# A product moved from VectorE to GpSimd and two mask matmuls from TensorE to VectorE, once in each of eight attention units

## The chip, the cores and the metric

The kernel runs on one core of a Trainium2 chip. The metric is the device time of one execution in microseconds (us); a comparison rests on the median of several runs. TensorE multiplies matrices, VectorE and GpSimd work elementwise, ScalarE does exponentials and copies, SyncE issues transfers. The engines run side by side and wait for one another through semaphores.

## What is computed

A block with a sparse or dense attention, a feed-forward layer, a second layer with an expert chosen per batch row, and a mixture of the best two of eight experts. Only the attention matters here. With these inputs it takes the sparse way, and every query's 32 key numbers lie below 256:

```python
Kg = K[:, :, idx]; Vg = V[:, :, idx]                       # 32 keys for each of 1024 queries
s_scores = jnp.einsum('bhsd,bhskd->bhsk', Q, Kg) * scale
s_scores = jnp.where(prior_index_mask[:Ss][None, None], s_scores, -jnp.inf)
sparse_out = jnp.einsum('bhsk,bhskd->bhsd', jax.nn.softmax(s_scores, axis=-1), Vg)
...
x = x + ffn(cond(x, ...))          # first layer
x = x + moe(experts(x, ...))       # second layer
```

Two batch rows, 1024 queries each, 16 heads of 16 numbers.

## The kernel before

The gather is turned into counting: for each query `few_W` holds how often each of the 256 keys occurs in its list (transposed, 128 keys on the partitions, two tiles of 1024 queries, bf16), and the probabilities are exp(score) times that count. `Mneg` is -1e30 where a count is zero (queries on the partitions, bf16); it keeps such keys out of the greatest score of a query.

The attention is cut into 8 units (2 batch rows x 4 groups of 4 heads), each with 8 jobs. `due()` (class `Few`) yields one list of steps that every engine goes through in the same order, each doing its own part. A job number counts for two kinds of work at different times. Guard job i, at time t = i, takes 128 queries and 4 heads: TensorE writes the scores of 2 heads x 256 keys into each of two banks of psG (L567) and adds `Mneg` with a second matmul against the unit matrix (L569); VectorE takes the negated maximum per head and query from each bank (L812) into column 48 of `few_Qa`. Bank p of guard i can be written when VectorE has reduced bank p of guard i - 1 (semaphore `g_max`; the first twelve guards use psS in turn with psG). Score job n, at time t = n + 12 (`LAG`), takes one head and one tile of 128 keys against 1024 queries: TensorE (L584) into psS, ScalarE's exp into slot n % 8 of `Pr` (L732), VectorE's "weigh" step (L820), which caps at 3e38 and multiplies by the counts in one instruction. The weigh step of job n - 1 stands in the list right after the guard of time t = n + 12. The values matmuls (L597), which read four slots of `Pr` at once, stand five jobs later ("values0", "values1").

So time t = 13 + 8u holds both guard 5 of a unit and the weigh step of the first job of unit u, one behind the other on VectorE.

Other work at these places: ScalarE's copy of the transposed queries (L724), which frees a bank of psM for TensorE's transposes (L618, L634); ScalarE's copies into `few_Qa` (L673, L674) and GpSimd's subtraction behind them (L440, step "fill"), twice in a unit; the normalization by VectorE once a unit (L830, L833); splits of weights into two parts on VectorE between the jobs (L1610); and GpSimd's L1902 near the end of the attention.

## Time and profile before

| | |
|---|---|
| median of 3 timed runs | 491.25 us (491.18 to 492.18) |
| profiled execution | 490.34 us, span 488.5 us, mean granted TensorE clock 0.994 |
| TensorE busy | 94% of the span |
| VectorE busy | 79% |
| ScalarE busy | 54% |
| GpSimd busy | 20% |
| attention: guards and scores | about 45 to 222 us of the span |

Rows of the trace give the start in us from the span's start, the duration, the engine (PE is TensorE, DVE is VectorE, ACT is ScalarE, POOL is GpSimd), the line, the operation and its operands (output<-inputs), and in brackets the idle time before with what ended it. xN means N instructions in a row. Ends of matmuls are modelled, so their starts are the better guide.

### The profile page before, as it was taken

The page shows a single profiled execution, that of the slowest core. Times are in us where ns is not written, and L with a number is a line of the kernel's source. Part 1 is how long each engine was busy: PE and PEld are TensorE (multiplying, and loading weights), DVE is VectorE, ACT ScalarE, POOL GpSimd, SP SyncE. Part 2 cuts the span into 40 slices and gives each one's busy share as a digit, 9 for nine tenths or more (in the row PEclk, how much of TensorE's full clock was granted, in tenths as well). Part 3 has the DMA queues.
Part 4 walks back from the last instruction along what each step waited for, and adds up shares of the span by engine and source line. Part 5 has one row for each costly group of instructions (what it writes and reads, how often), then busy time and mean ns, then how long its engine had stood idle before and what let it go on. Part 6 is the DMA issues. An engine that isn't in the chain of part 4 may idle for free.

```text
span 488.5 us, 7690 instructions
## 1 busy us (share of the span) xinstructions
PE 458.8 (94%) x2511; PEld 319.2 (65%) x2511; DVE 386.3 (79%) x760; ACT 261.4 (54%) x513; POOL 97.6 (20%) x102
## 2 busy tenths in 40 slices
PE   6999899999999999889999999999999999999990
PEld 3545554454555545436888888888888878899980
DVE  7998899999899989885976677657873779375376
ACT  4026588678769785874544544355343524465400
POOL 1003101101110122000100013300440024067744
PEclk9999999999999999999999999999999999999997
DMA  7700020999500000002241211111010102646357
GB/s 232 216 1 0 1 87 1 347 315 329 171 1 0 2 2 0 1 3 84 60 125 43 88 43 43 45 44 44 33 56 1 43 26 75 163 150 190 128 198 271
DMA packets 21536, 44.74 MB, mean 92 GB/s; under 512 B 7938, under 2 KB 14722, under 8 KB 21218
## 3 DMA queue, kind: packets, MB, share of 16 engines
q1 hardware_dynamic: 18850, 36.93, 24.3%
q0 software_dynamic: 2640, 7.24, 4.1%
q8 instruction: 24, 0.39, 0.4%
q14 instruction: 22, 0.18, 0.1%
HBM read 34.76 MB, written 23.00 MB: 118 GB/s over the span
## 4 chain that ended last, share of the span: by engine, by line
PE 71%; DVE 17%; ACT 3%; issue 3%; DMA 2%; POOL 1%; SPq 1%; DVEq 0%; ACTq 0%; POOLq 0%
DVE few_Qa L812 8%; PE psG L1697 5%; PE psG L1699 5%; PE psG L1698 5%; PE psS L1697 5%; PE psS L1699 5%; PE psS L1698 5%; PE psO L597 4%; DVE Pr L820 4%; PE psS L584 4%; PE psG L567 3%; PE psO L488 3%; PE psG L569 3%; PE psO L1697 2%; PE psO L1698 2%
## 5 line engine op out<-in xcount | busy, mean ns | idle before, releaser
L732 ACT ACTIVATE Pr<-psS 128x512 f32<-128x512 f32 x128 | 69.9, 602 | 33.2 <-PE psS L584 32.7
L820 DVE SCALAR_TENSOR_TENSOR Pr<-Pr,few_W 128x1024 f32<-128x1024 f32 x64 | 80.5, 1265 | 2.2 <-ACT Pr L732 2.1
L812 DVE TENSOR_REDUCE few_Qa<-psG 128x2 fp32r<-128x512 f32 x116 | 74.3, 681 | 5.6 <-PE psG L569 5.3
L567 PE MATMUL psG<-few_KG,QG 128*128 128x512 f32 x116 | 53.0, 500 | 3.1 <-DVE few_Qa L812 3.1
L584 PE MATMUL psS<-few_QAT,few_KP 128*128 128x512 f32 x128 | 48.1, 451 | 4.4 <-ACT Pr L732 2.9
L1960 DVE TENSOR_TENSOR hT_lo<-V,hT_hi 128x512 fp32r<-128x512 f32 x64 | 44.5, 695 | 2.2
L569 PE MATMUL psG<-Mneg,few_identb 128*128 128x512 bf16 x116 | 45.2, 390 | 0.0
L1958 DVE CAST hT_hi<-V 128x512 fp32r<-128x512 f32 x64 | 27.5, 429 | 19.7 <-ACT V L1883 12.6
L440 POOL TENSOR_TENSOR few_Qa<-Qn,few_Qa 128x256 fp32r<-128x256 f32 x16 | 16.4, 1025 | 124.9 <-ACT few_Qa L674 124.9
L584 PEld LDWEIGHTS psS<-few_QAT,few_KP 128*128 128x128 f32 x128 | 20.6, 189 | 26.7 <-issue 19.9
L1902 POOL TENSOR_TENSOR cT_lo<-attT,cT_hi 128x1024 fp32r<-128x1024 f32 x4 | 10.6, 2653 | 130.7 <-ACT cT_hi L1833 130.7
L1930 POOL DMA_INDIRECT expert_results<-block_out,block_rows x31 | 30.1, 971 | 26.6 <-ACT block_out L1864 19.6
L597 PE MATMUL psO<-Pr,few_VA 128*17 128x512 f32 x256 | 33.5, 598 | 0.4 <-DVE Pr L820 0.4
L567 PEld LDWEIGHTS psG<-few_KG,QG 128*128 128x128 f32 x116 | 22.3, 192 | 9.8 <-issue 7.1
L784 DVE TENSOR_SCALAR few_EQ<-few_idxb,cst 128x1024 f16<-128x1024 f16 x64 | 26.7, 476 | 1.8 <-ACT few_idxb L267 1.1
L569 PEld LDWEIGHTS psG<-Mneg,few_identb 128*128 128x128 bf16 x116 | 11.1, 96 | 25.3 <-issue 21.7
L1924 POOL DMA_INDIRECT expert_rows<-crow,place_in x24 | 25.0, 1041 | 7.7 <-issue 5.5
L1958 DVE CAST cT_hi<-V 128x512 fp32r<-128x512 f32 x8 | 3.4, 426 | 29.0 <-ACT V L1891 29.0
L724 ACT CAST few_QAT<-psM 128x512 fp32r<-128x512 f32 x32 | 19.1, 596 | 7.8 <-PE psM L552 7.8
L552 PE MATMUL psM<-cst,few_Qa 128*128 128x128 f32 x128 | 19.4, 274 | 0.5 <-DVE few_An L833 0.4
L1891 ACT ACTIVATE V<-psG,cbias 128x512 f32<-128x512 f32 x6 | 4.1, 689 | 26.4 <-PE psG L1699 26.4
L552 PEld LDWEIGHTS psM<-cst,few_Qa 128*128 128x128 f32 x128 | 15.6, 141 | 4.0 <-issue 2.0
(315 smaller groups left out, 1162.1 us busy)
## 6 DMA issues: line engine op xcount, KB each, us to landing
expert_rows<-blank_dram SPq DMA_DIRECT2D x8, 1548.0 KB, 24.0
block_rows<-expert_rows SPq DMA_DIRECT2D x31, 129.0 KB, 2.5
back<-expert_results SPq DMA_DIRECT2D x6, 512.0 KB, 6.7
staged<-w_dram SPq DMA_DIRECT2D x4, 512.0 KB, 4.5
x1T<-xT_dram SPq DMA_DIRECT2D x4, 512.0 KB, 4.0
staged<-ew_dram SPq DMA_DIRECT2D x4, 512.0 KB, 3.5
out_dram<-attT SPq DMA_DIRECT2D x6, 256.0 KB, 3.2
few_idxb<-entries_by_query SPq DMA_DIRECT2D x8, 128.0 KB, 4.3
```

The lines of the kernel that those rows point to most:

```text
L552: mm = nc.tensor.transpose(ps[:, p * 256 + j * P:p * 256 + j * P + P], self.Qa[:, f % SLOTS, st + j, 2 * p:2 * p + 2, :].rearrange("p h a ...
L567: nc.tensor.matmul(o, QG[:, (u // 2) % 2, st * P:st * P + P], self.KG[:, u % 2, 2 * p:2 * p + 2, :], start=True, stop=False)
L569: mm = nc.tensor.matmul(o, self.identb[:, :], Mneg[:, None, st * FEW_KEYS:(st + 1) * FEW_KEYS].to_broadcast([P, 2, FEW_KEYS]), start=False ...
L584: mm = nc.tensor.matmul(psS[:, f, :], self.KP[:, u % 2, j, r * P:r * P + P], self.QAT[:, u % 2, j // 2, q], start=True, stop=True)
L597: mm = nc.tensor.matmul(psO[VW * j:VW * j + VC, part, :], self.VA[:, b, r, h * VC:h * VC + VC], Pr[:, HG * r + j, 512 * part:512 * part + ...
L732: nc.scalar.activation(Pr[:, i % JOBS, 512 * f:512 * f + 512], psS[:, f, :], ACT.Exp, scale=SCALE).then_inc(self.s["s_exp"], 1)
L812: nc.vector.tensor_reduce(self.Qa[:, f % SLOTS, st, 2 * p:2 * p + 2, 48], self.guard_bank(i)[0][:, p, :].rearrange("p (h t) -> p h t", h=2 ...
L820: nc.vector.scalar_tensor_tensor(pr, pr, FMAX, self.W[:, r, :], ALU.min, ALU.mult).then_inc(self.s["s_prob"], 1)
L1697: nc.tensor.matmul(ps, w[0], a[1], start=start, stop=False)
L1698: nc.tensor.matmul(ps, w[1], a[0], start=False, stop=False)
L1699: return nc.tensor.matmul(ps, w[0], a[0], start=False, stop=stop)
L1960: nc.vector.tensor_tensor(tile.lo[at], v, tile.hi[at].bitcast(F32), ALU.subtract).then_inc(d["parts"], 1)
```

## The change

In each unit GpSimd does the weigh step of the first job, as two instructions: a minimum with 3e38 in place, then the product with the counts. The second waits for the first by a semaphore. The values matmuls wait for GpSimd's semaphore as well as VectorE's. And in the guards whose number is 5 modulo 8 TensorE leaves out the mask matmuls; VectorE adds `Mneg` and takes the maximum in one operation per head, four in a guard.

```diff
+BY_POOL = 0
+MASKED_BY_DVE = 5
+def weighed_before(n):
+    return n - (n + JOBS - 1 - BY_POOL) // JOBS
...
+                    if what == "weigh" and i % JOBS == BY_POOL:
+                        u = i // JOBS
+                        pool.wait_ge(self.s["s_exp"], 2 * (i + 1))
+                        pr = Pr[:, i % JOBS, :]
+                        nc.gpsimd.tensor_scalar(pr, pr, FMAX, None, ALU.min).then_inc(self.s["s_least"], 1)
+                        pool.wait_ge(self.s["s_least"], u + 1)
+                        nc.gpsimd.tensor_tensor(pr, pr, self.W[:, i % JOBS // HG, :],
+                                                ALU.mult).then_inc(self.s["s_prob_pool"], 1)
...
-                            nc.tensor.matmul(o, QG[:, (u // 2) % 2, st * P:st * P + P],
-                                             self.KG[:, u % 2, 2 * p:2 * p + 2, :], start=True, stop=False)
+                            mm = nc.tensor.matmul(o, QG[:, (u // 2) % 2, st * P:st * P + P], self.KG[:, u % 2, 2 * p:2 * p + 2, :],
+                                                  start=True, stop=st == MASKED_BY_DVE)
+                            if st == MASKED_BY_DVE:
+                                mm.then_inc(self.s["g_scores"], 1)
+                                continue
...
-                        pe.wait_ge(self.s["s_prob"], HG * (i + 1))
+                        pe.wait_ge(self.s["s_prob"], weighed_before(HG * (i + 1)))
+                        if r == BY_POOL // HG:
+                            pe.wait_ge(self.s["s_prob_pool"], u + 1)
...
+                            if i % JOBS == MASKED_BY_DVE:
+                                for h in range(2):
+                                    seen = self.guard_bank(i)[0][:, p, h * FEW_KEYS:(h + 1) * FEW_KEYS]
+                                    mm = nc.vector.tensor_tensor_reduce(
+                                        seen, seen, Mneg[:, MASKED_BY_DVE * FEW_KEYS:(MASKED_BY_DVE + 1) * FEW_KEYS], -1.0, FMAX,
+                                        ALU.add, ALU.min, self.Qa[:, f % SLOTS, st, 2 * p + h, 48:49])
+                                mm.then_inc(self.s["g_max"], 1)
+                                continue
...
-                    if what == "weigh":
+                    if what == "weigh" and i % JOBS != BY_POOL:
```

How the order of instructions changes. VectorE, around the sixth guard of a unit in the middle of the attention, before:

```order
L830 RECIPROCAL few_rden<-psM 128x32
L833 TENSOR_TENSOR few_An<-psM,few_rden 128x8x64
L812 TENSOR_REDUCE few_Qa<-psG 128x2 x2
L820 SCALAR_TENSOR_TENSOR Pr<-Pr,few_W 128x1024
L812 TENSOR_REDUCE few_Qa<-psG 128x2 x2
L820 SCALAR_TENSOR_TENSOR Pr<-Pr,few_W 128x1024
L812 TENSOR_REDUCE few_Qa<-psG 128x2 x2
L820 SCALAR_TENSOR_TENSOR Pr<-Pr,few_W 128x1024
```

The same place now (an ISA row with psG is one masked reduction, the one behind it writes its accumulator):

```order
L867 TENSOR_TENSOR few_An<-psM,few_rden 128x8x64
L846 TENSOR_REDUCE few_Qa<-psG 128x2 x2
L854 SCALAR_TENSOR_TENSOR Pr<-Pr,few_W 128x1024
L841 ISA psG,few_Qa<-psG,Mneg 128x256
L841 ISA few_Qa 128x1
L841 ISA psG,few_Qa<-psG,Mneg 128x256
L841 ISA few_Qa 128x1
L841 ISA psG,few_Qa<-psG,Mneg 128x256
L841 ISA few_Qa 128x1
L841 ISA psG,few_Qa<-psG,Mneg 128x256
L841 ISA few_Qa 128x1
L846 TENSOR_REDUCE few_Qa<-psG 128x2 x2
```

Two maxima and the product behind them have become eight instructions, and the next maxima follow at once.

GpSimd, in the attention (way21 is ScalarE's semaphore for the copies into few_Qa, way28 that of the exponentials, way31 that of the minimum), before:

```order
L440 TENSOR_TENSOR few_Qa<-Qn,few_Qa 128x16x16 [waits way21] x16
L1902 TENSOR_TENSOR cT_lo<-attT,cT_hi 128x1024 [waits at_hi]
L1902 TENSOR_TENSOR cT_lo<-attT,cT_hi 128x1024 [waits at_hi,attention_done]
```

And now, from the fifth unit's pair to the end:

```order
L452 TENSOR_SCALAR Pr<-Pr 128x1024 [waits way28]
L454 TENSOR_TENSOR Pr<-Pr,few_W 128x1024 [waits way31]
L459 TENSOR_TENSOR few_Qa<-Qn,few_Qa 128x16x16 [waits way21] x2
L452 TENSOR_SCALAR Pr<-Pr 128x1024 [waits way28]
L454 TENSOR_TENSOR Pr<-Pr,few_W 128x1024 [waits way31]
L459 TENSOR_TENSOR few_Qa<-Qn,few_Qa 128x16x16 [waits way21]
L1936 TENSOR_TENSOR cT_lo<-attT,cT_hi 128x1024 [waits at_hi]
L452 TENSOR_SCALAR Pr<-Pr 128x1024 [waits way28]
L454 TENSOR_TENSOR Pr<-Pr,few_W 128x1024 [waits way31]
L452 TENSOR_SCALAR Pr<-Pr 128x1024 [waits way28]
L454 TENSOR_TENSOR Pr<-Pr,few_W 128x1024 [waits way31]
L1936 TENSOR_TENSOR cT_lo<-attT,cT_hi 128x1024 [waits at_hi,attention_done]
```

The pairs stand behind a subtraction each, in the seventh unit behind the product for cT_lo.

TensorE, from the scores of slot 5 to the guard of slot 6 in a unit, before:

```order
L639 MATMUL psM<-cst,few_Kn 128x128 x2
L567 MATMUL psG<-few_KG,QG 128x512
L569 MATMUL psG<-Mneg,few_identb 128x512
L567 MATMUL psG<-few_KG,QG 128x512
L569 MATMUL psG<-Mneg,few_identb 128x512
L634 MATMUL psM<-cst,Qn 128x128 x4
L584 MATMUL psS<-few_QAT,few_KP 128x512 x2
L567 MATMUL psG<-few_KG,QG 128x512
```

And now:

```order
L663 MATMUL psM<-cst,few_Kn 128x128 x2
L586 MATMUL psG<-few_KG,QG 128x512 x2
L658 MATMUL psM<-cst,Qn 128x128 x4
L606 MATMUL psS<-few_QAT,few_KP 128x512 x2
L586 MATMUL psG<-few_KG,QG 128x512
```

The two masks are gone; the transposes of Qn (in other units of An) follow the guard directly.

## Rows read from the trace of the kernel before

**Rows 1.** The page's part 1: busy us, share of the span, instructions.

```profile
PE 458.8 (94%) x2511; PEld 319.2 (65%) x2511; DVE 386.3 (79%) x760; ACT 261.4 (54%) x513; POOL 97.6 (20%) x102
```

**Rows 2.** Busy time in one unit: stretch, length, engines, TensorE's clock, DMA.

```profile
134.80:156.14 21.34, 20.61 (x120) 10.89 (x120) 20.37 (x27) 16.57 (x37) 2.21 (x2) 1.00 0.00 1
```

**Rows 3.** The chain that ended last, at a unit's slots 0 and 1.

```profile
157.43 1.13 DVE Pr L820
...
159.31 0.47 PE psG L567
```

**Rows 4.** VectorE in order of time, slots 5, 6 and 0.

```profile
148.92 1.72 DVE L820 SCALAR_TENSOR_TENSOR Pr<-Pr,few_W 128x1024 f32<-128x1024 f32 x1
150.57 1.28 DVE L812 TENSOR_REDUCE few_Qa<-psG 128x2 fp32r<-128x512 f32 x2
151.77 1.21 DVE L820 SCALAR_TENSOR_TENSOR Pr<-Pr,few_W 128x1024 f32<-128x1024 f32 x1
...
156.14 1.29 DVE L812 TENSOR_REDUCE few_Qa<-psG 128x2 fp32r<-128x512 f32 x2 [0.60 <-PE psG L569]
...
177.60 1.29 DVE L812 TENSOR_REDUCE few_Qa<-psG 128x2 fp32r<-128x512 f32 x2 [0.22 <-PE psG L569]
```

**Rows 5.** TensorE in order of time, behind sixth guards of two units.

```profile
148.29 0.63 PE L634 MATMUL psM<-cst,Qn 128*128 128x128 f32 x4 [0.42 <-ACT few_QAT L724]
...
149.46 0.39 PE L569 MATMUL psG<-Mneg,few_identb 128*128 128x512 bf16 x1
...
170.15 0.63 PE L618 MATMUL psM<-cst,few_An 128*128 128x128 f32 x4 [0.80 <-ACT few_QAT L724]
```

**Rows 6.** VectorE's small instructions in order of time, before the attention.

```profile
4.80 0.16 DVE L207 TENSOR_SCALAR lam<-lam 128x2 f32<-128x2 f32 x1
...
11.53 0.41 DVE L769 TENSOR_TENSOR few_Kn<-psO,Pr 128x256 f32<-128x256 f32 x1
```

**Rows 7.** GpSimd: a fill; L1902's count, shortest, median and longest ns.

```profile
1.42 0.95 POOL L255 MEMSET few_Ka<- 128x1024 f32 x1
L1902 POOL TENSOR_TENSOR cT_lo<-attT,cT_hi x4: 2402/2412/3385, 189.4 to 341.2; 128x1024 fp32r<-128x1024 f32 x4
```

**Rows 8.** GpSimd in the attention, and VectorE's longest product.

```profile
138.67 1.48 POOL L440 TENSOR_TENSOR few_Qa<-Qn,few_Qa 128x256 fp32r<-128x256 f32 x1 [9.46 <-ACT few_Qa L674]
148.83 0.74 POOL L440 TENSOR_TENSOR few_Qa<-Qn,few_Qa 128x256 fp32r<-128x256 f32 x1 [8.68 <-ACT few_Qa L674]
170.69 1.31 POOL L440 TENSOR_TENSOR few_Qa<-Qn,few_Qa 128x256 fp32r<-128x256 f32 x1 [9.21 <-ACT few_Qa L674]
189.45 3.38 POOL L1902 TENSOR_TENSOR cT_lo<-attT,cT_hi 128x1024 fp32r<-128x1024 f32 x1 [6.51 <-ACT cT_hi L1833]
191.72 2.19 DVE L820 SCALAR_TENSOR_TENSOR Pr<-Pr,few_W 128x1024 f32<-128x1024 f32 x1
```

**Rows 9.** GpSimd's subtractions for few_Ka and a VectorE addition at the same time.

```profile
39.20 2.52 POOL L447 TENSOR_TENSOR few_Ka<-few_Kn,few_Ka 128x512 fp32r<-128x512 f32 x2 [36.56 <-DVE few_EQ L784]
40.31 0.42 DVE L765 TENSOR_TENSOR Qn<-psO,Pr 128x256 f32<-128x256 f32 x1 [0.92 <-PE psO L488]
```

**Rows 10.** The first two units: TensorE, VectorE and GpSimd in order of time.

```profile
59.86 0.69 PE L584 MATMUL psS<-few_QAT,few_KP 128*128 128x512 f32 x2 [1.34 <-DVE few_Qa L812]
64.45 0.74 POOL L440 TENSOR_TENSOR few_Qa<-Qn,few_Qa 128x256 fp32r<-128x256 f32 x1 [7.32 <-ACT few_Qa L674]
68.73 1.28 DVE L812 TENSOR_REDUCE few_Qa<-psG 128x2 fp32r<-128x512 f32 x2
74.22 0.46 PE L567 MATMUL psG<-few_KG,QG 128*128 128x512 f32 x1 [0.47 <-DVE few_Qa L812]
84.20 1.21 DVE L1610 TENSOR_TENSOR w_lo<-staged,w_hi 128x1024 fp32r<-128x1024 f32 x1
```

**Rows 11.** TensorE at guard 62, and VectorE at the attention's end.

```profile
191.35 0.47 PE L567 MATMUL psG<-few_KG,QG 128*128 128x512 f32 x1 [0.33 <-DVE few_Qa L812]
216.18 1.23 DVE L820 SCALAR_TENSOR_TENSOR Pr<-Pr,few_W 128x1024 f32<-128x1024 f32 x1 [0.24 <-ACT Pr L732]
```

More of the change, by code:

```diff
@@ L188, in bass_adaln_ffn @@
             "qg_full", "qg_out", "kt_full", "kt_out", "kg_ready", "k_copied", "k_twice", "ka_ready", "ka_full", "kp_out",
-            "q_hi", "q_lo", "g_scores", "g_max", "qa_full", "qat_out", "s_scores", "s_exp", "s_prob",
+            "q_hi", "q_lo", "g_scores", "g_max", "qa_full", "qat_out", "s_scores", "s_exp", "s_prob", "s_prob_pool", "s_least",
             "pv_done", "ot_out", "on_full", "recip", "on_out", "at_full", "at_out")
@@ L805, in vector @@
                         f, st = divmod(i, HALF)
+                        if i == MASKED_BY_DVE:
+                            dve.wait_ge(self.s["neg_out"], 2)
                         if f >= SLOTS and st % 2 == 0:
```

## The prediction

> **What bounds the kernel now.** I read the page's busy shares first, then the stretches, then the chain, then single engines. TensorE is busy 94% of the span, VectorE 79%, GpSimd 20% [rows 1]. The edit touches only the attention stage, from about 45 us to 222 us, and there the picture is closer: one unit of eight jobs lasts 21.34 us, in which TensorE is busy 20.61 us and VectorE 20.37 us [rows 2]. Two engines share the bound, coupled by the two psG banks: a guard matmul needs the bank that VectorE has reduced one job before. I call the eight jobs of a unit slots 0 to 7, by the guard that stands in them. The chain shows who is late where [rows 3]: VectorE in slot 0 (maxima, the product of 157.43 us) and the first half of slot 1 (one maximum, in the row left out), which releases TensorE at 159.31 us; from there to the next such place TensorE and ScalarE set the pace. The edit lies in slot 5: the product of a unit's first job and its sixth guard stand next to each other. VectorE reaches TensorE again only where it waits for it, 0.60 us before slot 0 in one unit and 0.22 us in the next [rows 4]. That slack is what the added work of slots 5 to 7 may use for nothing.
>
> **TensorE: two mask matmuls fewer in each unit.** A mask matmul lasts 0.39 us with its modelled end [rows 5], so at most 0.78 us of work goes, less since matmuls overlap. Nothing of it is a gain: right behind the sixth guard TensorE waits for ScalarE's copy of QAT, 0.42 us in one unit and 0.80 us in the next [rows 5], and that copy hangs on exponentials issued before the guard. The wait gets longer by what the masks took. Value 0, eight times. Were that wait not there, the gain would be at most 8 x 0.78 = 6.2 us.
>
> **VectorE: four masked reductions in place of two.** Two maxima take 1.20 us from start to start (150.57 to 151.77 [rows 4]). Each new instruction adds 128x256 from PSUM and from SBUF, and has a second instruction behind it that writes the accumulator. The nearest row for the first part is an addition of 128x256 from PSUM, 0.41 us; for the second, an instruction of 128x2, 0.16 us [rows 6]. So a pair costs between 0.41 us (each overlaps its predecessor by 0.08 us, as products do, 1.21 us long for a step of 1.13) and 0.57 us (each waits for the other); below nothing is out, since twice as many instructions go over as many elements. I take 0.50 us, the middle: 2.0 us for 1.20, **+0.8 us** in slot 5 (+0.4 to +1.1).
>
> **VectorE: one product fewer.** A product starts the next instruction 1.13 us later [rows 3]: **-1.13 us** in slot 5. Slot 5 gets 0.3 us shorter on VectorE.
>
> **GpSimd: two instructions more, and what they hold up.** In a unit's slot 5 they stand behind the subtraction for Qa (0.74 us [rows 8]). The second, a product of two SBUF inputs of 128x1024, has a very near row: L1902, 2.41 us in the median [rows 7]. The first, a minimum with a constant, isn't in the trace. The nearest rows are GpSimd's MEMSET of 128x1024, 0.95 us, which writes the same amount and reads nothing, and that product with one read more, 2.41 us [rows 7]. I take 1.0 us: the extra of the product over the fill seems to be its two reads. Ends 0.95 and 2.4 us. The wait of the second on the first I leave at nothing; it covers itself with the step to the next instruction.
> By time alone GpSimd is free for this: the values of a unit's first half come five jobs later, over 12 us, and the pair needs under 6. The price is elsewhere. Rows show that GpSimd's elementwise instructions and VectorE's products exclude one another: L1902, issued at 189.45 us just behind a product, took 3.38 us, and the product of 191.72 us took 2.19 us where the one of 151.77 us took 1.21 [rows 4]; the subtraction of 138.67 us took 1.48 us for 0.74 [rows 8]. A VectorE addition with one input in PSUM and one in SBUF wasn't held up beside GpSimd (0.42 us at 40.31 us, while GpSimd subtracts from 39.20 to 41.7 us [rows 9]), so maxima and masked reductions run on. The Trainium skill (SBUF — State Buffer, Who interferes with whom) says the same as a rule: a VectorE instruction with two SBUF inputs and a GpSimd instruction that reads SBUF block each other for a whole instruction, whichever comes first; the trace agrees (2.19 us). A sum that left it out would give VectorE 0.3 us back in each slot 5.
>
> **One unit, walked through** (before's times, around 148.8 us). The subtraction starts at 148.83 us and ends at 149.57 [rows 8]; minimum to 150.6, product to 153.0 us. VectorE: masked reductions 147.7 to 149.7; the maxima of slot 6 wait for TensorE's masks (the first of them runs from 149.46 to 149.85 us [rows 5]) and run from about 149.95 to 151.15. Now its product wants to start, and GpSimd holds it till 153.0. Then product, maxima, product: 153.0 + 1.13 + 1.20 + 1.13 = 156.45 us, where slot 0's maxima began at 156.14 [rows 4]: **+0.3 us**. In the other kind of unit (subtraction at 170.69 us, slot 0 at 177.60 [rows 4, 8]) the same walk is 170.69 + 0.74 + 1.0 + 2.41 + 3.46 = 178.3 us: **+0.7 us**. Slot 0 is on the chain, so both pass on whole. Third to sixth unit: 0.3 + 0.7 + 0.3 + 0.7 = **+2.0 us**.
>
> **The other places.**
> - Guard 5 (sixth of the first unit, before any product): maxima follow each other without a gap there and TensorE's first scores wait 1.34 us for them [rows 10]. **+0.8 us**, whole.
> - First unit, slot 5: VectorE has no gap here. Subtraction at 64.45 us, GpSimd's product ends at 64.45 + 0.74 + 1.0 + 2.41 = 68.6, VectorE's product at 69.7, while the next maxima began at 68.73 us. TensorE waits for VectorE at 74.22 us [rows 10]. **+1.0 us**.
> - Second unit: no gap either, and a split of weights (84.20 us [rows 10]) in slot 5, two SBUF inputs too, so the order is open. VectorE pays +0.8 - 1.13, a hold of 1.2 us (GpSimd's product begins with the maxima) to 2.4 us, and saves the 0.5 us for which the subtraction held a product here (as at 148.92 us, 1.72 long [rows 4]): +0.4 to +1.6. I take **+1.0 us**.
> - Seventh unit: TensorE waits 0.33 us for the first maximum of guard 61 [rows 11]; the first bank now comes free 2 x 0.50 - 0.60 = 0.4 us later, the second 0.8. **+0.6 us**. The 0.98 us that L1902 cost a product falls away with that product, but behind TensorE.
> - Last unit: VectorE has gaps here; GpSimd's product delays those of jobs 58 to 61; by a walk like the one above, the one that began at 216.18 us [rows 11] starts at 216.5: **+0.3 us**, before a VectorE stretch without gaps.
>
> Sum: 0.8 + 1.0 + 1.0 + 2.0 + 0.6 + 0.3 = **+5.7 us**. The profiled execution took 490.34 us (span 488.5), so 496.0 us; it lay 0.9 us under the median of the three timed runs. Against that median, 491.25 us, the forecast is **497.0 us**.
>
> **Rivals.**
> - A, the lock falls the other way: GpSimd's minimum takes over 1.55 us, so VectorE's product of slot 6 is issued before GpSimd's. Then GpSimd's product runs under the maxima of slot 7 and costs what the slack covers; walked as above: product of slot 6 from 151.15 us, GpSimd's from 152.3 to 154.7, product of slot 7 to 155.85, before 156.14 (no loss); in the other kind of unit it comes out at 177.7 for 177.60 (+0.1). The four middle units cost 0.2 in place of 2.0; the gapless ones about 1 each as before: +0.8 + 2.0 + 0.2 + 0.6 + 0.3 = +3.9, or 495.1 us; with cheap reductions (0.40 us a pair) 494. For it: the minimum has no row of its own. Against: its nearest row is 0.95 us.
> - B, **faster**: GpSimd's new instructions don't hold VectorE's products, and the accumulator pairs cost 0.40 us. Then slot 5 pays in the two gapless units, 2 x (-1.13 + 0.4) = -1.5 us, and the second unit's hold by the subtraction goes, -0.5; guards 5 and 61 cost 0.4 + 0.2. That is -1.4 us, 489.9 us against the median. It turns at a hold of some 0.7 us in each gapless unit. Against: the three holds of [rows 8]; for: none of them is by a GpSimd instruction with one input.
> - C, no change: no holds, but pairs of 0.50 us: 2 x (-1.13 + 0.8) - 0.5 + 0.8 + 0.6 = +0.2 us, 491.5 us. For and against as in B.
> - D, the accumulator pairs are dear: 0.75 us each. Then each slot 5 grows by 1.8 us, guard 5 costs 1.8, and TensorE's guard of slot 6 waits as well: about +10, 501 us. Against: an addition of 128x256 takes 0.41 us [rows 6].
> On A's open price there is a page: the Trainium skill (GPSIMD Engine Reference, Elementwise — side-by-side cycle accounting) gives 1.03 cycles per element at 1.2 GHz for short bodies, an estimate of 0.88 us for the minimum, and by it the middle units would cost 0.5 us less. No row of before shows it.
>
> **Chances.** Forecast (GpSimd first, 495 to 499.5 us with the ends of the unknown prices) 0.53; A 0.20; D 0.07; C 0.09; B 0.11. What a measurement of this kernel can tell from no change is about 0.2%, 1.0 us. Faster 0.11, same 0.09, slower 0.80. The range, 491 to 500 us, leaves out B and the top of D.
>
> **What would show it.** In the changed kernel's trace: (1) TensorE's wait for ScalarE's QAT copy behind the sixth guard near 0.9 and 1.25 us; (2) four masked reductions in 2.0 us; (3) GpSimd's minimum near 1.0 us and product near 2.4; (4) in slot 6 a VectorE product of some 3 us with GpSimd's beside it; (5) units of 21.7 to 22.1 us. A minimum above 1.55 us and a held product in slot 7 would be A; no long product anywhere would be B and prove the forecast wrong; so would units of 21.4 us in spite of the holds, if TensorE's chain turned out to be later than I read it.

## The result, and the profile after

The changed kernel takes 493.12 us (median of 22 runs, 491.86 to 495.51), the kernel before beside it 491.30 us (22 runs). The ratio is 1.0029, with a 95% interval of 1.0017 to 1.0041: slower, by 1.4 us (0.8 to 2.0; the two medians lie 1.8 us apart). The direction was forecast and the time lies in the range, but the forecast was +5.7 us.

To see where the time goes I measure the same places in each profile from one common start, VectorE's first maxima of the attention (45.28 us before, 45.20 us after), to its last pair of weight splits (217.33 us before). That is the whole attention stage, without what lies ahead of it and behind it. All "landmarks" below are such distances, taken from VectorE's rows in order of time.

```profile
45.20 1.28 DVE L846 TENSOR_REDUCE few_Qa<-psG 128x2 fp32r<-128x512 f32 x2
...
218.69 2.35 DVE L1644 TENSOR_TENSOR w_lo<-staged,w_hi 128x1024 fp32r<-128x1024 f32 x2
```

After: 218.69 - 45.20 = 173.49 us; before: 172.05 us. So the profiled attention stage got 1.44 us longer, which agrees with the timed runs. The two profiled executions as a whole differ by more, 490.34 and 493.69 us: another 2.0 us lie behind the last landmark, where the code is the same (more on it below). Landmarks in between (the maxima of guard 12 at 61.13 us before, the start of guard 21 at 83.00 us before, the reciprocal of each unit) divide the stage. The masks of guard 21, +0.29 us, count to the second unit, in whose slot 5 they stand:

| place | forecast | after less before |
|---|---|---|
| guard 5 | +0.8 | +0.30 |
| first unit | +1.0 | +0.28 |
| second unit | +1.0 | +0.18 |
| third to sixth unit | +2.0 | +0.03 |
| seventh unit | +0.6 | +0.25 |
| last unit | +0.3 | +0.40 |
| sum | +5.7 | +1.44 |

Part 1 of the page of after, answering to [rows 1] (busy us, share, instructions):

```profile
PE 456.5 (93%) x2495; PEld 317.9 (65%) x2495; DVE 382.6 (78%) x800; ACT 261.9 (53%) x513; POOL 139.4 (28%) x118
```

TensorE has 2.3 us less to do, VectorE 3.7 us less, and the kernel is slower. GpSimd has 41.8 us more. The unit in the middle, VectorE in order of time, the place of [rows 4] (CUSTOM_DVE_ANT_0 is a masked reduction, the row behind it writes its accumulator):

```profile
148.43 0.43 DVE L841 CUSTOM_DVE_ANT_0 psG<-psG,Mneg 128x256 f32<-128x256 f32 x1
148.77 0.14 DVE L841 DVE_READ_ACCUMULATOR2_ANT few_Qa<- 128x1 fp32r x1
148.77 0.47 DVE L841 CUSTOM_DVE_ANT_0 psG<-psG,Mneg 128x256 f32<-128x256 f32 x1
...
150.64 1.29 DVE L846 TENSOR_REDUCE few_Qa<-psG 128x2 fp32r<-128x512 f32 x2 [0.59 <-PE psG L591]
151.85 1.21 DVE L854 SCALAR_TENSOR_TENSOR Pr<-Pr,few_W 128x1024 f32<-128x1024 f32 x1
153.80 1.29 DVE L846 TENSOR_REDUCE few_Qa<-psG 128x2 fp32r<-128x512 f32 x2 [0.74 <-PE psG L591]
155.01 1.32 DVE L854 SCALAR_TENSOR_TENSOR Pr<-Pr,few_W 128x1024 f32<-128x1024 f32 x1
156.82 1.29 DVE L846 TENSOR_REDUCE few_Qa<-psG 128x2 fp32r<-128x512 f32 x2 [0.49 <-PE psG L591]
```

and GpSimd at the same place:

```profile
149.53 0.74 POOL L459 TENSOR_TENSOR few_Qa<-Qn,few_Qa 128x256 fp32r<-128x256 f32 x1 [8.68 <-ACT few_Qa L698]
150.24 2.77 POOL L452 TENSOR_SCALAR Pr<-Pr 128x1024 f32<-128x1024 f32 x1
153.09 2.15 POOL L454 TENSOR_TENSOR Pr<-Pr,few_W 128x1024 f32<-128x1024 f32 x1
```

Three things to read here. The masked reductions step by 0.38 us, not 0.50. GpSimd's minimum takes 2.77 us, not 1.0, and lies outside both of my ends (0.95 and 2.4). And VectorE's product of slot 6 starts at 151.85 us, 1.6 us after that minimum has begun, and takes 1.21 us as ever: the minimum isn't holding it. By the time GpSimd's product starts (153.09), VectorE's is out, and the two maxima of slot 7 run under it. Only the end of GpSimd's product touches VectorE's next one, 1.32 us in place of 1.21. VectorE then waits 0.49 us for TensorE at slot 0. This is the order of the rival A.

In the first two units VectorE has hardly a gap (two waits for TensorE of 0.2 us each in the first), and there products are held. VectorE in slots 6 and 7 of the second unit, and GpSimd beside it:

```profile
86.13 1.28 DVE L846 TENSOR_REDUCE few_Qa<-psG 128x2 fp32r<-128x512 f32 x2
87.33 1.56 DVE L854 SCALAR_TENSOR_TENSOR Pr<-Pr,few_W 128x1024 f32<-128x1024 f32 x1
88.81 1.28 DVE L846 TENSOR_REDUCE few_Qa<-psG 128x2 fp32r<-128x512 f32 x2
90.01 2.83 DVE L854 SCALAR_TENSOR_TENSOR Pr<-Pr,few_W 128x1024 f32<-128x1024 f32 x1
```

```profile
86.77 2.77 POOL L452 TENSOR_SCALAR Pr<-Pr 128x1024 f32<-128x1024 f32 x1
89.62 2.14 POOL L454 TENSOR_TENSOR Pr<-Pr,few_W 128x1024 f32<-128x1024 f32 x1
```

The product of 90.01 us is held until GpSimd's has ended (89.62 + 2.14 = 91.76; it is done 1.1 us later). The product of 87.33 us starts 0.56 us into the minimum and is 0.35 us longer than 1.21: held up to 0.9 us into a minimum of 2.77 us, and not to its end at 89.54 us. That second kind of hold is the news of this case.

TensorE behind the sixth guard, the place of [rows 5]:

```profile
148.99 0.63 PE L658 MATMUL psM<-cst,Qn 128*128 128x128 f32 x4 [0.88 <-ACT few_QAT L748]
...
170.84 0.63 PE L642 MATMUL psM<-cst,few_An 128*128 128x128 f32 x4 [1.25 <-ACT few_QAT L748]
```

0.42 and 0.80 us have become 0.88 and 1.25 us: the masks that TensorE no longer does turned into a wait for ScalarE, as forecast.

### The profile page after: what moved, and what is told of

Its sections match the earlier page's. It is cut to its first block, busy times and chain, and to the rows that moved or that the text cites. A ratio compares the mean times of both kernels' runs of the same rounds, so it can differ in the third digit from the quotient of the medians.

```text
span 491.9 us, 7729 instructions
## 1 busy us (share of the span) xinstructions
PE 456.5 (93%) x2495; PEld 317.9 (65%) x2495; DVE 382.6 (78%) x800; ACT 261.9 (53%) x513; POOL 139.4 (28%) x118
## 4 chain that ended last, share of the span: by engine, by line
PE 71%; DVE 17%; issue 3%; ACT 3%; DMA 2%; POOL 2%; SPq 0%; DVEq 0%; ACTq 0%; POOLq 0%
DVE few_Qa L846 7%; PE psG L1731 5%; PE psG L1733 5%; PE psG L1732 5%; PE psO L621 5%; PE psS L1731 5%; PE psS L1733 4%; PE psS L1732 4%; DVE Pr L854 4%; PE psS L606 4%; PE psG L586 3%; PE psO L507 3%; PE psG L591 3%; PE psO L1731 2%; PE psO L1732 2%
## 5 line engine op out<-in xcount | busy, mean ns | idle before, releaser
L854 DVE SCALAR_TENSOR_TENSOR Pr<-Pr,few_W 128x1024 f32<-128x1024 f32 x56 | 73.5, 1320 | 1.8 <-ACT Pr L756 1.7
L846 DVE TENSOR_REDUCE few_Qa<-psG 128x2 fp32r<-128x512 f32 x102 | 65.5, 683 | 10.7 <-PE psG L591 10.6
L586 PE MATMUL psG<-few_KG,QG 128*128 128x512 f32 x116 | 51.5, 491 | 4.1 <-DVE few_Qa L846 3.4
L591 PE MATMUL psG<-Mneg,few_identb 128*128 128x512 bf16 x102 | 39.7, 390 | 0.0
L606 PEld LDWEIGHTS psS<-few_QAT,few_KP 128*128 128x128 f32 x128 | 20.6, 189 | 27.6 <-issue 20.8
L1958 POOL DMA_INDIRECT expert_rows<-crow,place_in x24 | 26.3, 1096 | 7.7 <-issue 5.5
L452 POOL TENSOR_SCALAR Pr<-Pr 128x1024 f32<-128x1024 f32 x8 | 22.8, 2856 | 9.2 <-ACT Pr L756 9.2
L591 PEld LDWEIGHTS psG<-Mneg,few_identb 128*128 128x128 bf16 x102 | 9.7, 96 | 22.1 <-issue 19.9
```

The lines of the kernel that those rows point to most:

```text
L586: mm = nc.tensor.matmul(o, QG[:, (u // 2) % 2, st * P:st * P + P], self.KG[:, u % 2, 2 * p:2 * p + 2, :], start=True, stop=st == MASKED_BY ...
L591: mm = nc.tensor.matmul(o, self.identb[:, :], Mneg[:, None, st * FEW_KEYS:(st + 1) * FEW_KEYS].to_broadcast([P, 2, FEW_KEYS]), start=False ...
L606: mm = nc.tensor.matmul(psS[:, f, :], self.KP[:, u % 2, j, r * P:r * P + P], self.QAT[:, u % 2, j // 2, q], start=True, stop=True)
L846: nc.vector.tensor_reduce(self.Qa[:, f % SLOTS, st, 2 * p:2 * p + 2, 48], self.guard_bank(i)[0][:, p, :].rearrange("p (h t) -> p h t", h=2 ...
L854: nc.vector.scalar_tensor_tensor(pr, pr, FMAX, self.W[:, r, :], ALU.min, ALU.mult).then_inc(self.s["s_prob"], 1)
```

## Experiments

Two questions: is the loss in the masks or in the product, and which of GpSimd's two instructions holds VectorE, for how long? Later a third: is there time in TensorE's masks anywhere else? The spans and landmarks are of one profiled execution each; the ratios are timed runs against the kernel before on the same chip.

### One half of the change at a time

```diff
-MASKED_BY_DVE = 5                      # pool_only: every mask by TensorE again
+def masked_by_dve(i): return False
```

> The product of each unit's first job by GpSimd (minimum, then product), the mask matmuls left with TensorE in all guards. Theory 1 (the holds fall where VectorE has slack: the minimum, 2.77 us in the changed kernel's trace, lets VectorE's product of slot 6 go first): the four middle units cost nothing, the first two about nothing to 0.4 us together, the last unit 0.4; VectorE's split of weights that began at 217.33 us before begins at 217.5 to 218.1; ratio 1.000 to 1.002. Theory 2 (the holds cost as much as was predicted, some 0.5 us a unit, and the masks that TensorE no longer does pay it back): units of 21.8 us, that split at 219.5 to 221, ratio 1.004 to 1.008.

```diff
-                    if what == "weigh" and i % JOBS == BY_POOL:    # mask_only: every product by VectorE
+                    if what == "weigh" and False:
```

> Only the masked reductions of each unit's sixth guard by VectorE, all products by VectorE. Theory 1: TensorE's saved matmuls lengthen its wait for the QAT copy and gain nothing; four pairs of 0.38 us for 1.20 cost 0.33 us each at guard 5 and in the two gapless units, 0.2 at guard 61, nothing in the middle: the split of 217.33 us at 218.2 to 218.5, ratio 1.001 to 1.003. Theory 2: TensorE's saving counts, 0.3 to 0.5 us a unit: the split at 214.5 to 216, ratio 0.993 to 0.998.

| | attention stage, less before | timed ratio (95%) |
|---|---|---|
| product only | +0.28 | 1.0022 (1.0004 to 1.0039) |
| masks only | +1.15 | 1.0052 (1.0039 to 1.0064) |
| both (the change) | +1.44 | 1.0029 (1.0017 to 1.0041) |

In the profiles the halves add up to the change (0.28 + 1.15 = 1.43). The masks cost 0.30 us at each of guard 5, the first and the second unit, nothing in the third to sixth and 0.25 us in the seventh. The product costs nothing before the last unit (0.09 us up to guard 21, -0.05 us up to the reciprocal behind it): in the gapless first two units the 1.13 us taken off VectorE and what GpSimd's two instructions hold cancel. In the last unit it costs 0.3 to 0.4 us. VectorE in pool_only, beside [rows 11]:

```profile
208.19 1.54 DVE L864 SCALAR_TENSOR_TENSOR Pr<-Pr,few_W 128x1024 f32<-128x1024 f32 x1 [0.44 <-ACT Pr L766]
210.31 7.71 DVE L864 SCALAR_TENSOR_TENSOR Pr<-Pr,few_W 128x1024 f32<-128x1024 f32 x5 [0.59 <-ACT Pr L766]
```

Five products in 7.71 us, where free ones, 1.13 us apart, would need 5.7: GpSimd's product (from 210.46 us, 3.08 long) falls among them. The 2.0 us more are covered for the most part, since before VectorE waits for ScalarE four times between its last products (as in [rows 11]).

The timed ratios of the halves are larger than their landmarks, by 0.8 and 1.4 us, and don't add up: 1.1 and 2.6 us for the halves, 1.4 us for both. The profiles show no such loss in the attention, and it stays open (more on it below, at the masks in slots 6 and 7). So the split between the halves rests on one profile of each.

### The minimum: left out, and cut short

```diff
-                        nc.gpsimd.tensor_scalar(pr, pr, FMAX, None, ALU.min).then_inc(self.s["s_least"], 1)
-                        pool.wait_ge(self.s["s_least"], u + 1)
```

> The changed kernel without GpSimd's minimum (the cap at 3e38 of these eight products is left out); its product follows the subtraction at once. Theory 1: the product of 2.14 us holds VectorE's product of slot 6 by some 0.5 us, which the wait for TensorE before slot 7 covers; in the first two units it holds less than in the changed kernel; the last unit's delay goes too. The split of 217.33 us (before), 218.69 (changed) at 216.8 to 217.8; ratio 0.998 to 1.001. If GpSimd's product costs by its mere 2.1 us of hold wherever it stands: 218.7 or later.

```diff
-                        nc.gpsimd.tensor_scalar(pr, pr, FMAX, None, ALU.min).then_inc(self.s["s_least"], 1)
+                        nc.gpsimd.tensor_scalar(pr[:, 0:352], pr[:, 0:352], FMAX, None, ALU.min).then_inc(self.s["s_least"], 1)
```

> The changed kernel with the minimum over 352 of 1024 columns, some 1.0 us as the prediction took it (the cap is left out for the other columns). It puts GpSimd's product back where the prediction had it, in front of VectorE's product of slot 6. The prediction's walk with the measured 2.14 us product: slot 0 later by 0.0 and 0.4 us in turn in the middle units, first unit +0.7, second +0.5, guard 5 +0.3: the split of 217.33 us at 219.0 to 220.5, ratio 1.003 to 1.007. If the order of the two products does not matter: as the changed kernel, 218.7 or less.

Without the minimum the attention stage is 0.30 us longer than before (+0.28 at guard 5, -0.07 and -0.17 in the first two units, +0.25 in the seventh, none in the last) and the ratio is 1.0003 (0.9984 to 1.0022). So the minimum makes 1.1 us of the change's 1.4, in the first, second and last unit.

Cut to 352 of 1024 columns it takes 1.09 us, nearly the 1.0 us that I had assumed, and the kernel gets much slower: attention stage +5.27 us, ratio 1.0148 (1.0120 to 1.0176). A shorter instruction costs more. VectorE and GpSimd in the middle unit of that kernel:

```profile
153.11 1.29 DVE L856 TENSOR_REDUCE few_Qa<-psG 128x2 fp32r<-128x512 f32 x2 [0.60 <-PE psG L601]
154.31 2.78 DVE L864 SCALAR_TENSOR_TENSOR Pr<-Pr,few_W 128x1024 f32<-128x1024 f32 x1
```

```profile
152.68 1.09 POOL L462 TENSOR_SCALAR Pr<-Pr 128x352 f32<-128x352 f32 x1
153.86 2.16 POOL L464 TENSOR_TENSOR Pr<-Pr,few_W 128x1024 f32<-128x1024 f32 x1
```

This is the picture that the prediction drew: GpSimd's product has gone first, and VectorE's product of slot 6 lasts 2.78 us. The third to sixth unit cost 0.07, 0.74, 0.04 and 0.73 us here, where the walk said 0.3 and 0.7 in turn. So the walk had the mechanism of this order right. That its size fits as well is in part luck: with the measured 2.14 us for GpSimd's product the same walk gives 0.0 and 0.4, as expected above, and 0.3 us of every second unit stay unexplained. The first unit costs 0.76 us (+1.0 forecast, +0.7 expected); the second gains 1.06, since there VectorE's product gets in first again (90.24 us, GpSimd's at 90.86). Most of the rest, 3.7 us, falls in the seventh unit and is a second race of the same kind. Before, GpSimd's L1902 starts 0.06 us after a product of VectorE (189.45 [rows 8], the product at 189.39 us) and waits for it. Here, VectorE and then GpSimd:

```profile
193.31 3.21 DVE L864 SCALAR_TENSOR_TENSOR Pr<-Pr,few_W 128x1024 f32<-128x1024 f32 x1
```

```profile
193.07 2.38 POOL L1946 TENSOR_TENSOR cT_lo<-attT,cT_hi 128x1024 fp32r<-128x1024 f32 x1 [7.68 <-ACT cT_hi L1877]
```

GpSimd is 0.24 us ahead; VectorE's product is held to 3.21 us, and TensorE behind it waits 2.52 us for psG, up to 197.45 us, where it waits 0.52 us in the changed kernel. That is 2.0 us. Right behind the wait TensorE's granted clock falls to half (third number from the end) for about 3.3 us:

```profile
198.00:199.00 1.00, 1.00 (x3) 0.55 (x3) 0.65 (x3) 0.00 (x0) 1.00 (x1) 0.50 0.00 0
200.00:201.00 1.00, 1.00 (x8) 0.15 (x8) 1.00 (x2) 0.00 (x0) 0.00 (x0) 0.50 0.00 0
```

From the matmul of 197.45 us to the next guard TensorE takes 4.92 us, for 3.45 in the changed kernel at full clock: another 1.5 us. Neither the prediction nor the expectation had either.

### A minimum running all the time

```diff
+                    if what == "weigh" and i < 44:          # the kernel before, and on GpSimd:
+                        pool.wait_ge(self.s["s_exp"], 2 * (i + 1))
+                        pool.wait_ge(self.s["idle"], i + 1)
+                        nc.gpsimd.tensor_scalar(self.idle[:, :], self.idle[:, :], FMAX, None, ALU.min).then_inc(self.s["idle"], 1)
```

> The kernel before, with a GpSimd minimum of an unused tile of 128x768 at the place of each of the first 44 weigh steps, so that such minima meet VectorE's products at many phases; nothing reads them. If GpSimd's one-input minimum holds VectorE's products only in a first part (0.9 us of 2.77 for 1024 columns in the changed kernel, so some 0.7 of 2.1 here), products that start later than 0.7 us into a minimum last 1.21 us, and the longest product is near 1.9 us. If it holds them for its whole length, products of up to 3.3 us appear and those that start late in a minimum are lengthened too. If it holds nothing, all are at 1.21 us but those beside the subtraction.

If a minimum held VectorE's products for its whole length, 44 of them close behind one another would lengthen the attention by far more than the 0.41 us that they cost over the whole stage. VectorE and GpSimd in a stretch where neither rests:

```profile
104.88 1.21 DVE L826 SCALAR_TENSOR_TENSOR Pr<-Pr,few_W 128x1024 f32<-128x1024 f32 x1
...
109.55 1.34 DVE L826 SCALAR_TENSOR_TENSOR Pr<-Pr,few_W 128x1024 f32<-128x1024 f32 x1
```

```profile
103.03 2.13 POOL L442 TENSOR_SCALAR few_idle<-few_idle 128x768 f32<-128x768 f32 x1 [0.15 <-POOL few_idle L442]
105.32 2.77 POOL L442 TENSOR_SCALAR few_idle<-few_idle 128x768 f32<-128x768 f32 x1 [0.16 <-POOL few_idle L442]
...
108.98 2.13 POOL L442 TENSOR_SCALAR few_idle<-few_idle 128x768 f32<-128x768 f32 x1
```

The product of 104.88 us starts 1.85 us into a minimum and takes 1.21 us. The one of 109.55 us starts 0.57 us into one and takes 1.34: held to 0.70 us into it. At 1024 columns the hold ended 0.9 us in (above). In this run eight products start within the first 0.6 us of a minimum, and each is held up to 0.68 to 0.70 us into it; those that start 0.73 to 2.27 us into one take 1.21 or 1.22 us. 0.70 / 768 and 0.9 / 1024 are both 0.9 ns a column, so at these two widths the hold is a third of the instruction. The other way round it works too: the minimum of 105.32 us starts within a product and takes 0.64 us longer. The durations (1.09 us for 352 columns, 2.13 for 768, 2.77 for 1024) make 2.5 ns a column and 0.2 us; GpSimd's product with two inputs needs 2.14 us for 1024. The instruction with one input less is the slower one, and holds VectorE the less.

The timed ratio is 1.0059 (1.0027 to 1.0090), 2.9 us, much more than 0.41. A part of that the profile shows: TensorE's granted clock in three stretches at the attention's end (TensorE's share of full speed is the third number from the end):

```profile
210.00:215.00 5.00, 4.02 (x22) 1.18 (x14) 4.02 (x4) 4.03 (x9) 0.00 (x0) 1.00 0.00 0
215.00:220.00 5.00, 4.59 (x20) 1.16 (x20) 4.51 (x5) 3.31 (x7) 0.00 (x0) 0.66 0.00 0
220.00:225.00 5.00, 5.00 (x32) 3.25 (x32) 3.96 (x6) 1.37 (x2) 0.00 (x0) 0.99 0.63 209
```

A clock of 0.66 over 5 us is 3.4 us at 1.2 in place of 2.4 GHz. The attention's end (first matmul of aoT_lo) then comes 1.53 us later than before, where the last split still was 0.41 late. The other 1.4 us of the timed 2.9 stay open.

### Masks where VectorE has slack

The change put the masks on VectorE in slot 5. In slots 6 and 7 VectorE waits before slot 0 (0.60 and 0.22 us [rows 4]), masked reductions cost only 0.38 us a head for 0.30, and what TensorE saves in slot 7 stands behind ScalarE's QAT copies. Both kernels are the kernel before with another set of guards:

```diff
+def masked_by_dve(i): return i in (31, 39, 47, 55)              # mask7_late
+def masked_by_dve(i): return i in (31, 38, 39, 47, 54, 55)      # mask_where_slack, slack_again
```

> Masked reductions by VectorE in guards 31, 39, 47 and 55 (slot 7 of the four units in which VectorE waits for TensorE there), nothing else changed. Theory 1 (what counts is the slot: behind slot 5's guard TensorE waits anyway, before slot 0 it is the later engine): slot 0 begins 0.47 us earlier in two units (no longer than TensorE's two masks) and about 0.2 us earlier in the other two, where VectorE is then the later one: attention 1.1 to 1.4 us shorter, ratio 0.997 to 0.998. Theory 3 (TensorE's masks never count, being hidden everywhere): attention unchanged or up to 1.3 us longer.

> As the last one, and guards 38 and 54 (slot 6 of the two units in which VectorE waits 0.41 us for TensorE there). Theory 1: 0.47 us in two units and 0.7 us in the other two, attention 2.0 to 2.4 us shorter, ratio 0.995 to 0.996. Theory 3: unchanged or up to 2 us longer.

The attention stage is 1.15 and 2.06 us shorter, as expected; with six guards the units last 20.8 and 20.95 us for 21.3 and 21.5. The timed ratios are 0.9996 (0.9976 to 1.0015) and 1.0001 (0.9985 to 1.0017): nothing, where 0.995 to 0.998 was expected. The profile of mask_where_slack, its clock in the same stretches as above:

```profile
210.00:215.00 5.00, 3.83 (x16) 1.33 (x16) 3.77 (x5) 4.03 (x9) 0.00 (x0) 0.99 0.00 0
215.00:220.00 5.00, 5.00 (x24) 1.50 (x24) 4.66 (x4) 2.48 (x5) 0.00 (x0) 0.67 0.02 7
```

Ahead of the fall TensorE had waited for ScalarE's exponentials three times, 0.23 to 0.60 us each, from 209.96 to 214.56 us. Up to the first matmul of aoT_lo the gain has shrunk from 2.06 to 1.02 us (mask7_late: from 1.15 to 0.08, with 0.86 and 0.80 in its two stretches). Before has the same waits and no fall. So I asked whether the fall belongs to the kernel and can be filled away, on another chip, with two spare mask matmuls into an idle psG bank where TensorE waits:

```diff
+                            if f == 0 and i in (57, 61, 62):
+                                pe.wait_ge(self.s["g_max"], 2 * UNITS * JOBS)
+                                for _ in range(2):
+                                    nc.tensor.matmul(psG[:, 0, :].rearrange("p (h t) -> p h t", h=2), self.identb[:, :],
+                                                     Mneg[:, None, 0:FEW_KEYS].to_broadcast([P, 2, FEW_KEYS]), start=True, stop=True)
```

> The kernel before, with two spare bf16 mask matmuls (128x512, about 0.23 us each from start to start) into an idle psG bank ahead of the score jobs 57, 61 and 62 of the last unit, where TensorE waits 0.57 to 0.61 us for ScalarE. Theory (the waits there come ahead of a fall of the granted clock in some executions): the mean granted clock rises from 0.991 and the time falls by up to 0.5 us. Rival (the clock has nothing to do with it): no change of clock, time equal within 0.2%. Both leave the attention's landmarks where they were (last w_lo pair 172.05 us after the first maxima, within 0.2).

> The masks of guards 31, 38, 39, 47, 54 and 55 on VectorE, and the spare matmuls. Without them this edit gained 2.06 us up to the last w_lo pair, and only 1.02 us up to the first matmul of aoT_lo, since TensorE's clock was granted at 0.50 from 215 to 218.8 us; timed it gained nothing. Theory (clock): no stretch at 0.50 near 215 us, the gain at aoT_lo is 1.8 to 2.1 us, mean clock 0.991 or more, time 0.3 to 0.4% under before. Rival (the gain is lost in the later stage, 400 us and on): clock cured, gain at aoT_lo 2 us, time still within 0.1% of before.

> The same masks without the spare matmuls, on the chip and beside the runs of the others. Clock theory: mean granted clock 0.0025 below before's again, time about 1 us above the version with spare matmuls, within 0.2% of before. Rival: the two versions are equal in time.

| | attention stage, less before | at aoT_lo | mean clock | timed ratio (95%) |
|---|---|---|---|---|
| spare matmuls only | -0.08 | -0.09 | 0.9912 | 1.0000 (0.9983 to 1.0016) |
| masks and spare matmuls | -2.15 | -2.15 | 0.9887 | 0.9977 (0.9964 to 0.9990) |
| masks again, without them | -2.14 | -2.14 | 0.9875 | 0.9977 (0.9958 to 0.9995) |

(The mean clock is of 12 runs each; the 35 runs of before beside them had 0.9895. This chip takes 499.45 us for the kernel before, 7 to 9 us more than the others, but the attention's landmarks of the first row are those of before within 0.1 us.) The very same kernel that showed the fall on the first chip has a full clock here:

```profile
215.00:220.00 5.00, 5.00 (x30) 3.14 (x28) 4.90 (x6) 1.77 (x3) 0.00 (x0) 1.00 0.35 104
```

and keeps its 2.14 us at the attention's end. So the fall is not fixed by the kernel's order. With and without the spare matmuls the time is equal: the clock theory's expectation (1 us between the two) failed, and so did the mean clock of 0.991 or more. The spare matmuls do nothing measurable to the time, though the mean clock is a little higher with them (0.9912 for 0.9895, 0.9887 for 0.9875). Whether they would fill away a fall was not tested: this chip's profile of the masks without them has none there. What stays of the mask edit is 0.23% on this chip (0.05 to 0.42%; 0.10 to 0.36% with the spare matmuls), half of the 2.1 us in the profile, and nothing measurable on the first one. It is still the one version here, with the next, that beat the kernel before anywhere.

The other half I can only place, not explain. From the last landmark to the end every kernel runs the same code, and the profiled executions differ there by up to 5 us (271.2 us before, 273.2 us in the changed kernel, 276.0 us in no_min; on the last chip all are longer). TensorE's first wait for the experts' rows, in mask_where_slack and in no_min:

```profile
419.13 0.41 PE L1791 MATMUL psM<-cst,block_rows 128*128 128x128 f32 x2 [1.01 <-DMA block_rows<-expert_rows]
```

```profile
418.79 0.41 PE L1789 MATMUL psM<-cst,block_rows 128*128 128x128 f32 x2 [1.69 <-DMA block_rows<-expert_rows]
```

Before, the largest such wait is 0.28 us, at 417.75 us, in the changed kernel 0.78 us, at 418.85 us, and up to the matmul for x_lo at 402 us nothing has changed since the attention's end (178.1 to 178.2 us in before, mask_where_slack and no_min). One profile of each can't say whether an earlier or later attention causes it, or chance. A lower clock is a second candidate: the mean granted clock of the masked kernels lies 0.0008 to 0.0027 under that of before beside them, on both chips. But the two versions on the last chip, with and without spare matmuls, differ by 0.0012 in it and not in time.

### The measured prices put together

```diff
+UNITS_OF_POOL = (2, 3, 4, 5)                                    # GpSimd's product in four units only
+def masked_by_dve(i): return i in (30, 31, 38, 39, 46, 47, 54, 55)
```

> The measured prices put to use: in the third to sixth unit GpSimd takes the first product (VectorE 1.13 us less, GpSimd's minimum 2.77 us, its product under the maxima of slot 7), and VectorE masks slots 6 and 7 there (8 pairs at 0.38 us, +0.66 us for the unit) where it had slack, so TensorE is 1.56 us of mask matmuls lighter; spare matmuls as before. Theory (two coupled engines, both must get lighter): units of 20.2 to 20.8 us for 21.27 and 21.53, the last w_lo pair 2.5 to 4 us earlier, time 0.4 to 0.8% under before. Rival (ScalarE's exponentials or the hold of VectorE's products by GpSimd's product end it): no better than 2.0 us at the w_lo pair.

The attention stage is 1.68 us shorter (units of 20.7 and 21.4 us), ratio 0.9972 (0.9953 to 0.9992): a gain, but less in the profile than with the masks alone (2.15), and not the 2.5 to 4 us that I expected. VectorE in slots 5 and 6 and TensorE there:

```profile
125.55 1.28 DVE L861 TENSOR_REDUCE few_Qa<-psG 128x2 fp32r<-128x512 f32 x2
128.21 0.43 DVE L856 CUSTOM_DVE_ANT_0 psG<-psG,Mneg 128x256 f32<-128x256 f32 x1 [1.38 <-PE psG L596]
...
132.44 1.60 DVE L869 SCALAR_TENSOR_TENSOR Pr<-Pr,few_W 128x1024 f32<-128x1024 f32 x1
```

```profile
126.71 0.63 PE L657 MATMUL psM<-cst,few_An 128*128 128x128 f32 x4 [0.80 <-ACT few_QAT L763]
```

The product taken off VectorE in slot 5 becomes a wait of 1.38 us, since TensorE stands before slot 6 waiting for ScalarE's QAT copy whatever VectorE does. Behind that wait come the dearer masked reductions and a product held by GpSimd's (1.60 us). The fourth and the sixth unit show it best: there the masked guards are those of the masks alone, and with GpSimd's product the gain falls from 0.6 to 0.2 us a unit. Here, work taken off an engine in front of a wait and put on it behind the wait is a loss. The rival's number held (no better than 2.0 us), and one of its two reasons, the hold by GpSimd's product, is there with 0.39 us; the other was the wrong work of ScalarE, the exponentials and not the QAT copy.

## Why the prediction was right or wrong

**Right.** The masks on TensorE are worth nothing where they were left out: the QAT wait grew to 0.88 and 1.25 us, as said (0.9 and 1.25). VectorE's maxima and masked reductions run on beside GpSimd. VectorE's and GpSimd's products exclude each other for nearly the whole instruction (2.83 us at 90.01 us, 2.78 us in the kernel with the short minimum: held up to 2.0 us into GpSimd's 2.14). The loss from masks at guard 5 and in the seventh unit, and from GpSimd in the last one, lies where it was said.

**Wrong, first of all: the minimum's price, and with it the order in slot 6.** The prediction took 1.0 us, with ends of 0.95 and 2.4 us. It was 2.77 us, above the upper end. The nearest row was chosen by the amount written (the MEMSET of [rows 7]), and the extra of the product was put down to its reads; the product with two reads as an upper end seemed safe, and was not. What decides is the length at which VectorE's product of slot 6 gets in ahead of GpSimd's, 1.55 us by the rival A, and the minimum lies beyond it. So the order is A's: middle units +0.03 us where the forecast said +2.0 and A +0.2. That is 2.0 of the 4.3 us by which the sum was too high. The kernel with a minimum of 1.09 us shows the forecast's order, and 1.58 us in those four units. That the measured time lies within 491 to 500 us is no merit of the walk: the range was wide enough to hold A and C as well.

**Wrong: that every elementwise instruction of GpSimd holds VectorE's products.** I let them be held with its whole length. The three holds of [rows 8] were all between instructions with two inputs, which rival B noted; the two cases without holds, B and C, I weighed at 0.20. The minimum holds for 0.9 us of 2.77. The Trainium skill (SBUF — State Buffer, Who interferes with whom) calls the shared pair of ports an exclusive lock, and says of VectorE's two-port modes that whoever issues first has it "for the whole instruction"; for the two products the trace agrees (2.0 of 2.14 us), for GpSimd's one-input minimum the measurement decides against it (0.9 of 2.77 us).

**Wrong in size.** A masked reduction with its second instruction steps by 0.38 us (148.77, 149.15, 149.53 us), below my lower end of 0.41: guard 5 cost +0.30 and not +0.8. GpSimd's product takes 2.14 us, not 2.41. First unit: -1.13 us for the product, +0.3 for the masks, one product held by 0.75 us (69.68 us, 1.96 long), a hold of 0.2 us by the subtraction that falls away (74.59 us before, 1.42 long), and some 0.6 us for the two waits for TensorE: +0.28 for +1.0. Second unit: -1.13 for the product, +0.33 for the masks, +0.35 and +1.62 for the holds, and two holds by the subtraction fall away, of 0.54 us each (before: products of 1.75 us at 85.33 and 95.20 us; I had counted one): +0.1 by this sum, +0.18 measured, for +1.0. Seventh unit: +0.25 for +0.6, by the cheaper pair.

**The rivals.** A had the mechanism of the middle units, and its walk fits the trace within 0.1 us (VectorE's product of slot 6 starts 1.6 us into the minimum, GpSimd's after it); its sum (+3.9, "494 with cheap reductions") was still too high by the same sizes in the first two. No case had masks and holds both cheap with the order of A, which is what came: the prices went wrong together, all to one side, and the sum was wrong by 4.3 us.

## What to carry over

Where two engines lock each other out, the order in which their instructions meet can be worth more than their length: a GpSimd instruction cut from 2.77 to 1.09 us made this kernel's attention 3.8 us longer, 1.5 us of it by a half clock behind the wait that the new order made. So price an unseen instruction before its place, and if its ends straddle a point where the order turns, give both orders a like chance. And take work off an engine only where it is late. Here the masks taken off TensorE gave nothing in slot 5, ahead of a wait, and some 0.5 us of attention a unit in slots 6 and 7, of which the timed runs show half on one chip and nothing on another.

## What the runs showed of the hardware

- GpSimd's minimum with a constant, f32, in place: 1.09 us for 128x352, 2.13 us for 128x768, 2.77 us for 128x1024, longer than its product of two inputs (2.14 us for 128x1024). The Trainium skill (GPSIMD Engine Reference, Elementwise — side-by-side cycle accounting) would give the minimum 0.88 us by an estimate from its 1.03 cycles per element for short bodies; the trace doesn't agree as to duration, though the stretch for which it holds VectorE, 0.9 us, comes out near it. That the two are connected is only a guess.
- It holds a VectorE product for the first third of its time (0.70 us at 768 columns, 0.9 us at 1024) and is itself held by one that runs (2.13 to 2.77 us).
- A masked reduction of 128x256 takes 0.42 to 0.47 us and its accumulator read 0.14 us, but the next one starts 0.34 to 0.38 us after the last: the read runs beside it.
- The same kernel had TensorE's clock at half for some 3.3 us at the attention's end in one profiled execution and at full in another, on another chip, behind the same waits for ScalarE (0.2, 0.6 and 0.6 us).
